# A depthwise convolution split between VectorE and GpSimd: chunks 4 to 6 on GpSimd, two taps a slot on VectorE

## The chip, the core and the metric

The kernel runs on one core of one Trainium2 chip. The metric is device time in microseconds (us) of one launch, the median of three runs. The core's engines are TensorE (PE in the profile), VectorE (DVE), ScalarE (ACT), GpSimd (POOL) and SyncE (SP), which issues the DMAs. Each has its own instruction stream; they meet at semaphores alone.

## What is computed

Input x has 16 images of 128 channels and 56x56 pixels, float32. Four layers follow one another, each on the group-normalised x and added to it: a whitening, a deformable convolution (L1), window attention (L2) and a masked 3x3 convolution (L3). The change is in the first steps of L1:

```python
# L1, on x = group_norm(x), N,C,H,W = 16,128,56,56
xproj = inp @ in_w + in_b
x1 = conv_general_dilated(x, dw_w, (1, 1), pad 1, feature_group_count=C)   # depthwise 3x3
x1 = transpose(x1, (0, 2, 3, 1)) + dw_b
mu = x1.mean(-1); var = ((x1 - mu) ** 2).mean(-1)
x1 = gelu((x1 - mu) / sqrt(var + LN_EPS) * ln_g + ln_b)
offset = x1 @ off_w + off_b;  mask = softmax(x1 @ mask_w + mask_b)
out = sample xproj at the offsets, weighted by the mask, @ out_w + out_b
```

In the depthwise convolution each channel is convolved with nine taps of its own.

## The kernel before

An image lies in SBUF with its 128 channels on the partitions and its 3136 pixels along them. It is worked on in 7 chunks (`CHUNKS`) of 8 rows, that is 448 pixels (`CH`).

After a preface (covariance and power iteration, some 500 us), image 0 goes through its first steps alone. Then a loop of 15 turns follows; turn `i` overlaps two images. Its first half is the window stage of image `i` (`windows(i, i + 1)`): 32 slots (`PAIRS`), each with two attention windows on all engines, in an order written out by hand. Between the steps of a slot stand, by slot number, the first steps of image `i + 1`. Its second half is the sampling of image `i + 1` (`sample_tiles`) with the last steps of image `i` between. A last window stage, of image 15, has no next image.

In a window slot VectorE does, in this order: `before_first` (steps of the next image), `shift` (a row maximum and a subtraction of 128x800 from PSUM, lines 1815 and 1817), `turned` (a copy of 128x512 from PSUM, 1824), `normalise` (1831, 1833), `queries_keys` (a copy of 128x400 from PSUM, 1809), `before_last`. TensorE waits for VectorE's copies within the slot, and VectorE for TensorE's results.

The next image's first steps by slot: group norm in slots 2 to 4; its result `vp` (58x58 with a border of zeros) is written by ScalarE in slots 3 to 6, two chunks a slot (line 1135, signal `v1_in`); the projection `xproj` in slots 8 to 11 (PE line 702, VectorE line 1754 the slot after); the depthwise convolution on VectorE; then TensorE takes the channel mean off (`centred`, line 720) in the slots of `CT_AT`, ScalarE copies and squares the result (1115, 1116), the variance follows in slot 18 (`VAR_AT`), the rows go out in slots 20 to 23.

The depthwise convolution is `depthwise(n, j)`, with `j` from 0 to 35. It has four blocks (`DW_BLOCKS`) of two chunks, the last of one: 896, 896, 896 and 448 elements a partition. In each block tap 0 is a `tensor_scalar` (line 1773) from `vp` to `x1c`, and taps 1 to 8 are `scalar_tensor_tensor` (1775): `x1c = vp * w + x1c`, with both tensors in SBUF. `DW_SLOTS` gives three taps to each of the slots 5 to 16: one after `shift`, one after `turned`, one after `queries_keys` (`depthwise_of`, places 0, 1, 2). The block's last tap raises `dw_d`, on which `centred` waits.

GpSimd only writes constants: `zero_windows(i)` at the start of a window stage, `zero_taps` at slots 28 and 32 (line 557, an image's first two tap tables) and in the sampling (561). For image 0 it writes its two tap tables right after the image buffer is zeroed. `Chain` is a helper that raises an engine's own semaphore at each step and waits for it.

Of the kernel before, what the change touches and what calls it, by code (L numbers as in the profile page):

```python
# [8 lines left out]
ALU = mybir.AluOpType  # L9
# [3 lines left out]
N, C, H, W = 16, 128, 56, 56  # L13
PIX = H * W
# [5 lines left out]
G1, P9, CG = 16, 9, 8  # L20
ROWS = 8
CHUNKS = H // ROWS
# [26 lines left out]
TWO = (CHUNKS + 1) // 2  # L49
DW_BLOCKS = (CHUNKS + 1) // 2  # L50
DW_SLOTS = (5, 5, 5) + (6, 6, 6) + (7, 7, 7) + (8, 8, 8) + (9, 9, 9) + (10, 10, 10) + (11, 11, 11) + (12, 12, 12) + (13, 13, 13) + (14, 14, 14) + (15, 15, 15) + (16, 16, 16)
CT_AT = {12: (0, 1), 13: (2, 3), 15: (4, 5), 17: (6,)}

# [60 lines left out]
def build(nc, a):  # L114
    with ExitStack() as ctx:
# [3 lines left out]
        def sem(name):  # L119
            return ctx.enter_context(nc.semaphore(name))  # L120
# [137 lines left out]
        cv = carver(G_AT)  # L258
        x1c = cv(PIX)
        var_rows, sd_rows = cv(CH), cv(CH)  # L260
        sdt = [cv(CH).rearrange("c (t p) -> c t p", t=T4) for _ in range(4)]
# [27 lines left out]
        def sig(name, per=1, prime=PRIME):  # L289
            signals.append(Signal(sem(name), per, prime))  # L290
            return signals[-1]
# [4 lines left out]
        d_init, d_a, d_cov, d_pow, d_pre, d_main, d_blk, d_end = (sem(f"dve_own_{k}") for k in range(8))  # L296
        t_main = sem("act_own_main")

# [21 lines left out]
        cp_col, cp_img = sig("columns_copied", 2 * TY * 16), sig("rows_copied", 2 * 16)  # L320
        dw_d = sig("dw_taps", DW_BLOCKS)
        dw_p, dw_s = sig("dw_psum", CHUNKS), sig("dw_sbuf", CHUNKS)
# [39 lines left out]
        def dw_block(b):  # L362

            return range(2 * b, min(2 * b + 2, CHUNKS))
# [7 lines left out]
        def alone(eng):  # L372
            eng.sem_inc(s_passed, 1)
# [163 lines left out]
        def _(pool):  # L537
# [25 lines left out]
            def zero_windows(i):  # L563
# [11 lines left out]
                for u in range(2):  # L575
                    nc.gpsimd.memset(e_sb[u][:, :, NTOK:], 0.0).then_inc(l2_z.sem, 1)

            zero_taps(None, 0)
            with pool.Fori(0, N - 1) as i:
                zero_windows(i)  # L580
                zero_taps(i, i + 1)
            zero_windows(N - 1)

        @block.tensor
        def _(pe):
# [132 lines left out]
            def centred(n, k, bank):  # L718
                pe.wait_ge(dw_d.sem, dw_d.at(n, k // 2 + 1))
                nc.tensor.matmul(ps[:, bank, 0:CH], centre, x1c[:, k * CH:(k + 1) * CH], start=True, stop=True  # L720
                                 ).then_inc(dw_p.sem, 1)
# [1356 lines left out]
```

## Time and profile before

| what | before |
|---|---|
| time, median of 3 runs | 9815.72 us (9799.69 to 9819.58) |
| the profiled execution | 9807.95 us |
| its span on the core | 9806.1 us |
| busy in the span | PE 82%, DVE 75%, PEld 46%, ACT 40%, POOL 2% |
| granted clock of TensorE, mean | 0.907 |
| first of the 32 slots of the 16 window stages | 864, 1437, 2010, ..., 9435 us |

The profile is of one execution. PE is TensorE's matmuls, PEld its weight loads, beside them. Busy shares are averages over the whole span; in a single stage another engine can be the one that never waits. The chain is followed back from the last instruction, at each step to what released it. A slot is taken here from the start of one copy of line 1824 to the start of the next, so that it holds the second half of one slot's VectorE work and the first half of the next one's.

### The profile page before, as it was taken

Reading aid. Unit: us, or ns where it says so; the run is one execution under the profiler, and the core shown is the slowest. Engines: PE = TensorE matmul, PEld = TensorE weight load, DVE = VectorE, ACT = ScalarE, POOL = GpSimd, SP = SyncE. Lnnn points to the kernel's source line nnn. Section 1 sums busy time; section 2 is a strip of 40 time slices with the busy share of each in tenths; the row PEclk is TensorE's granted clock in tenths of the full one; section 3 lists DMA queues with packets and bytes.
Section 4 is the critical chain, followed back from the end, with each engine's and each line's share of the span. In section 5 each row is a group of like instructions: output and inputs, shape, how many; then the busy total and the mean of one; then the engine's idle time right before and its main releaser. Section 6 shows DMA issues by size and latency. Waiting matters only on the chain.

```text
span 9806.1 us, 288571 instructions
## 1 busy us (share of the span) xinstructions
PE 8025.1 (82%) x123582; PEld 4502.0 (46%) x123582; DVE 7400.9 (75%) x8865; ACT 3946.4 (40%) x6124; POOL 191.2 (2%) x253
## 2 busy tenths in 40 slices
PE   6458888887888888798888878888887988888797
PEld 5324445354444545444453534445353444535354
DVE  2478778868777886878788687878868787886863
ACT  0034435354343535434353533435353343535332
POOL 0000000000000000000000000000000000000000
PEclk7579999998999999899999989999998999999898
DMA  4000201111020111112011111201111110111101
GB/s 116 0 20 22 58 23 48 31 46 42 28 59 23 48 31 46 42 30 58 23 48 30 47 42 32 59 21 47 31 47 42 31 57 22 47 31 46 42 26 53
DMA packets 231836, 391.50 MB, mean 40 GB/s; under 512 B 26736, under 2 KB 168016, under 8 KB 223312
## 3 DMA queue, kind: packets, MB, share of 16 engines
q1 hardware_dynamic: 230544, 372.67, 13.5%
q8 instruction: 1006, 16.48, 0.7%
q14 instruction: 286, 2.34, 0.1%
HBM read 190.38 MB, written 130.55 MB: 33 GB/s over the span
## 4 chain that ended last, share of the span: by engine, by line
PE 58%; DVE 23%; issue 12%; ACT 6%; DVEq 1%; DMA 0%; SPq 0%; POOL 0%; ACTq 0%; POOLq 0%
PE ps L895 11%; PE ps L694 8%; PE ps L760 7%; DVE arena L1720 5%; PE ps L995 4%; PE ps L793 4%; PE ps L985 3%; PE ps L809 3%; PE ps L768 3%; DVE arena L1775 3%; PE ps L716 3%; PE ps L782 2%; DVE arena L1697 2%; DVE arena L1815 1%; DVE arena L1703 1%
## 5 line engine op out<-in xcount | busy, mean ns | idle before, releaser
L895 PE MATMUL ps<-arena,ident 64*64 64x512 f32 x5600 | 1752.1, 679 | 650.3 <-DVE arena L1720 650.1
L897 PE MATMUL ps<-arena,ident 48*64 48x512 f32 x5600 | 1756.0, 680 | 0.0
L1720 DVE TENSOR_TENSOR arena<-arena 112x2560 f32<-112x2560 f32 x560 | 1578.1, 2819 | 95.8 <-PE ps L897 89.3
L895 PEld LDWEIGHTS ps<-arena,ident 64*64 64x64 f32 x5600 | 490.2, 148 | 1686.8 <-issue 1678.0
L760 PE MATMUL ps<-arena,wqk 128*128 128x400 f32 x2048 | 888.3, 551 | 156.1 <-DVE arena L1824 114.4
L694 PE MATMUL ps<-vp,convw 128*128 128x448 f32 x2016 | 822.8, 550 | 23.6 <-ACT vp L1316 23.6
L1703 DVE TENSOR_TENSOR arena<-arena 112x576 f32<-112x576 f32 x1008 | 764.2, 758 | 34.9
L809 PE MATMUL ps<-arena 64*64 64x33 f32 x32768 | 636.7, 226 | 118.5 <-issue 64.5
L1237 ACT ACTIVATE arena<-ps 112x864 f32<-112x864 f32 x224 | 199.2, 889 | 1273.1 <-PE ps L716 1268.4
L793 PE MATMUL ps<-ident,arena 128*128 128x128 f32 x4096 | 575.1, 285 | 142.6 <-ACT arena L1116 43.3
L1815 DVE TENSOR_REDUCE arena<-ps 128x16 f32<-128x800 f32 x512 | 504.9, 986 | 245.3 <-PE ps L782 241.6
L1809 DVE COPY arena<-ps 128x400 f32<-128x400 f32 x512 | 292.8, 572 | 520.8 <-PE ps L760 520.6
L809 PEld LDWEIGHTS ps<-arena 64*64 64x64 f32 x32768 | 567.4, 139 | 218.6 <-issue 217.6
L1697 DVE TENSOR_TENSOR arena<-arena 112x1728 f32<-112x1728 f32 x336 | 655.2, 1950 | 0.2 <-DVE arena L1685 0.2
L768 PE MATMUL ps<-wv,arena 128*64 128x256 f32 x4096 | 572.3, 401 | 37.6 <-ACT arena L1185 37.5
L760 PEld LDWEIGHTS ps<-arena,wqk 128*128 128x128 f32 x2048 | 321.4, 191 | 611.8 <-ACT arena L1172 220.5
L1179 ACT ACTIVATE arena<-arena 128x800 f32<-128x800 f32 x512 | 447.1, 873 | 370.8 <-DVE arena L1817 366.9
L694 PEld LDWEIGHTS ps<-vp,convw 128*128 128x128 f32 x2016 | 365.6, 190 | 457.6 <-issue 433.9
L782 PEld LDWEIGHTS ps<-arena 32*64 32x64 f32 x32768 | 403.0, 135 | 330.9 <-issue 323.1
L793 PEld LDWEIGHTS ps<-ident,arena 128*128 128x128 f32 x4096 | 456.6, 145 | 189.5 <-issue 121.2
L1185 ACT ACTIVATE arena<-ps 128x512 f32<-128x512 f32 x512 | 305.5, 597 | 590.1 <-PE ps L793 589.7
L1775 DVE SCALAR_TENSOR_TENSOR arena<-vp,cols,arena 128x896 f32<-128x896 f32 (+1 forms) x512 | 525.1, 1026 | 1.0
(299 smaller groups left out, 12428.4 us busy)
## 6 DMA issues: line engine op xcount, KB each, us to landing
windows_out<-arena SPq DMA_DIRECT2D x1024, 100.0 KB
arena<-windows_out SPq DMA_DIRECT2D x224, 256.0 KB, 3.9
arena<-windows_out SPq DMA_DIRECT2D x224, 192.0 KB, 3.3
arena<-in_wqk SPq DMA_DIRECT2D x16, 2048.0 KB, 8.2
arena<-in_x_t SPq DMA_DIRECT2D x16, 1568.0 KB, 10.4
arena<-in_x SPq DMA_DIRECT2D x16, 1568.0 KB, 7.3
arena<-arena SPq DMA_DIRECT2D x32, 784.0 KB
out_x<-xb SPq DMA_DIRECT2D x112, 224.0 KB, 2.0
```

The source lines that it names most:

```text
L694: mm = nc.tensor.matmul(ps[:, bank, 0:CH], weights[:, tap, :], vp[:, ROWS * k + dy:ROWS * k + dy + ROWS, dx:dx + W], start=(tap == 0), sto ...
L760: nc.tensor.matmul(ps[:, 5 - m % 2, 0:NWY * NTOK], wqk[:, m * C:(m + 1) * C], xwb[b % 2][:, :, 0:NTOK], start=True, stop=True).then_inc(qk ...
L768: mm = nc.tensor.matmul(ps[hh * SLOT:(hh + 1) * SLOT, 4, wi * 256:(wi + 1) * 256], xwb[b % 2][:, 2 * pr + wi, :], wv[:, hh * 256:(hh + 1) ...
L793: mm = nc.tensor.transpose(ps[:, 4 + q, k * C:(k + 1) * C], e_sb[u][:, 8 * q + 2 * k:8 * q + 2 * k + 2, :], ident)
L809: mm = nc.tensor.matmul(ps[wi * SLOT:(wi + 1) * SLOT, 6 + hh, (kk * 4 + r) * VD:(kk * 4 + r + 1) * VD], et[u][hh * SLOT:(hh + 1) * SLOT, a ...
L895: nc.tensor.matmul(ps[half, 3, :], ident[0:SLOT, 0:SLOT], prod[0:SLOT, ring(c, dy), dx, :], start=(s < 2), stop=(s >= TAPS - 2), skip_grou ...
L897: mm = nc.tensor.matmul(ps[half, 4, :], ident[SLOT:PT, SLOT:], prod[SLOT:PT, ring(c, dy), dx, :], start=(s < 2), stop=(s >= TAPS - 2), ski ...
L1697: ownm.step(V.tensor_tensor(tt[0:PT, :].rearrange("p (a n) -> p a n", a=3), hat[0:PT, :, 0, :], hat[0:PT, bb, 1:2, :].to_broadcast([PT, 3, ...
L1703: ins = V.tensor_tensor(k5, k5, tt[0:PT, aa * HN:(aa + 1) * HN].rearrange("p (x y n) -> p x y n", x=3, y=3), ALU.add)
L1720: V.tensor_tensor(prod[0:PT, ring(c, dy), :, :].rearrange("p k (n e) -> p k n e", e=CG), taps.to_broadcast([PT, SHIFTS, N64, CG]), for_tap ...
L1775: ins = V.scalar_tensor_tensor(acc, around, dww[:, tap:tap + 1], acc, ALU.mult, ALU.add)
L1815: ownb.step(V.tensor_reduce(mxs[u].rearrange("p (r m) -> p r m", r=4), sv, AX.X, ALU.max))
```

## The change

- VectorE keeps blocks 0 and 1 (chunks 0 to 3): 18 taps, two a slot, in slots 5 to 13. Places 0 and 1 are used; nothing stands at place 2.
- GpSimd does blocks 2 (chunks 4 and 5) and 3 (chunk 6) in a new function `depthwise(n)`. It has no multiply and add in one instruction there: a tap is a `tensor_scalar` multiply of `vp` into a scratch tile `dw_part`, then a `tensor_tensor` add of it to `x1c`. That is 9 multiplies and 8 adds a block, 34 instructions an image, each waiting for the one before. It waits for `v1_in` of all seven chunks, and raises `dw_g` at a block's end.
- In GpSimd's stream it stands between `zero_windows(i)` and `zero_taps(i, i + 1)`; for image 0 it stands ahead of `zero_taps(None, 0)`.
- `centred` waits for `dw_d` in chunks 0 to 3 and for `dw_g` in chunks 4 to 6. The centring of chunks 2 and 3 moves from slot 13 to slot 14.

```diff
-DW_BLOCKS = (CHUNKS + 1) // 2
-DW_SLOTS = (5, 5, 5) + (6, 6, 6) + ... + (16, 16, 16)
-CT_AT = {12: (0, 1), 13: (2, 3), 15: (4, 5), 17: (6,)}
+DW_BLOCKS, DW_POOL = 2, 2
+DW_SLOTS = (5, 5, 6, 6, 7, 7, 8, 8, 9) + (9, 10, 10, 11, 11, 12, 12, 13, 13)
+CT_AT = {12: (0, 1), 14: (2, 3), 15: (4, 5), 17: (6,)}
...
+        dw_part = arena[:, G_AT + PIX:G_AT + PIX + 2 * CH]
...
+            def depthwise(n):
+                own_dw.turn(n, 34 - DW_POOL)
+                for b in range(DW_BLOCKS, DW_BLOCKS + DW_POOL):
+                    ks = dw_block(b)
+                    rows, size = ROWS * len(ks), CH * len(ks)
+                    acc = x1c[:, ks[0] * CH:ks[0] * CH + size].rearrange("c (h w) -> c h w", w=W)
+                    part = dw_part[:, 0:size].rearrange("c (h w) -> c h w", w=W)
+                    pool.wait_ge(v1_in.sem, v1_in.at(n, min(ks[-1] + 2, CHUNKS)))
+                    alone(pool)
+                    for tap in range(P9):
+                        dy, dx = tap // 3, tap % 3
+                        around = vp[:, ROWS * ks[0] + dy:ROWS * ks[0] + dy + rows, dx:dx + W]
+                        own_dw.step(nc.gpsimd.tensor_scalar(part if tap else acc, around, dww[:, tap:tap + 1], None, ALU.mult))
+                        alone(pool)
+                        if tap:
+                            ins = nc.gpsimd.tensor_tensor(acc, acc, part, ALU.add)
+                            if tap == P9 - 1:
+                                ins.then_inc(dw_g.sem, 1)
+                            else:
+                                own_dw.step(ins)
+                                alone(pool)
+
+            own_dw = Chain(pool, t_dw)
+            depthwise(0)
             zero_taps(None, 0)
             with pool.Fori(0, N - 1) as i:
                 zero_windows(i)
+                depthwise(i + 1)
                 zero_taps(i, i + 1)
...
             def centred(n, k, bank):
-                pe.wait_ge(dw_d.sem, dw_d.at(n, k // 2 + 1))
+                if k // 2 < DW_BLOCKS:
+                    pe.wait_ge(dw_d.sem, dw_d.at(n, k // 2 + 1))
+                else:
+                    pe.wait_ge(dw_g.sem, dw_g.at(n, k // 2 + 1 - DW_BLOCKS))
```

## Rows read from the trace of the kernel before

**Rows 1.** The page: busy time by engine, and the shares of the chain that ended last.
```profile
PE 8025.1 (82%) x123582; PEld 4502.0 (46%) x123582; DVE 7400.9 (75%) x8865; ACT 3946.4 (40%) x6124; POOL 191.2 (2%) x253
...
PE 58%; DVE 23%; issue 12%; ACT 6%; DVEq 1%; DMA 0%; SPq 0%; POOL 0%; ACTq 0%; POOLq 0%
```

**Rows 2.** Slots 5, 7-9, 11-15, last stage: length; busy PE, PEld, DVE, ACT, POOL.
```profile
3759.84:3767.47 7.63, 6.00 (x152) 3.80 (x148) 7.28 (x10) 4.34 (x8) 0.00 (x0) 1.00 0.10 30
...
3775.00:3781.95 6.95, 6.51 (x156) 4.17 (x152) 6.72 (x9) 4.34 (x6) 0.00 (x0) 1.00 0.12 35
3781.95:3790.59 8.64, 7.33 (x162) 5.66 (x164) 8.47 (x11) 5.04 (x7) 0.00 (x0) 1.00 0.09 26
3790.59:3799.33 8.74, 7.82 (x167) 5.66 (x164) 8.48 (x11) 4.78 (x6) 0.00 (x0) 1.00 0.09 27
...
3807.39:3815.52 8.13, 7.23 (x165) 5.12 (x164) 7.87 (x10) 2.93 (x5) 0.00 (x0) 1.00 0.10 31
3815.52:3823.81 8.29, 7.21 (x152) 4.20 (x150) 7.27 (x9) 4.78 (x8) 0.00 (x0) 1.00 0.09 27
3823.81:3831.49 7.68, 7.00 (x144) 3.83 (x141) 6.58 (x10) 4.19 (x8) 0.00 (x0) 1.00 0.10 29
3831.49:3838.74 7.25, 5.69 (x150) 3.70 (x143) 5.97 (x10) 3.63 (x7) 0.00 (x0) 1.00 0.22 46
3838.74:3847.70 8.96, 7.63 (x174) 4.66 (x173) 5.97 (x10) 4.78 (x9) 0.00 (x0) 1.00 0.60 103
...
9434.66:9615.44 180.78, 167.08 (x4448) 113.01 (x4444) 120.13 (x179) 82.39 (x132) 0.00 (x0) 1.00 0.13 37
```

**Rows 3.** VectorE's timeline around slot 7: start us, us, engine, line, operation.
```profile
3773.83 1.14 DVE L1775 SCALAR_TENSOR_TENSOR arena<-vp,cols,arena 128x896 f32<-128x896 f32 x1
3775.00 0.69 DVE L1824 COPY arena<-ps 128x512 f32<-128x512 f32 x1
3775.61 1.14 DVE L1775 SCALAR_TENSOR_TENSOR arena<-vp,cols,arena 128x896 f32<-128x896 f32 x1
```

**Rows 4.** Groups by shape, VectorE: count, busy us, mean ns, idle before.
```profile
L1775 DVE SCALAR_TENSOR_TENSOR arena<-vp,cols,arena 128x896 f32<-128x896 f32 x384 | 438.6, 1142 | 0.7
...
L1775 DVE SCALAR_TENSOR_TENSOR arena<-vp,cols,arena 128x448 f32<-128x448 f32 x128 | 86.5, 676 | 0.3
...
L1773 DVE TENSOR_SCALAR arena<-vp,cols 128x896 f32<-128x896 f32 x48 | 32.5, 677 | 2.1 <-ACT vp L1135 2.1
```

**Rows 5.** Groups by shape, GpSimd.
```profile
L561 POOL MEMSET arena<- 112x1600 f32 x80 | 114.5, 1431 | 3705.6 <-DVE arena L1720 3705.6
...
L576 POOL MEMSET arena<- 128x224 f32 x32 | 8.1, 286 | 0.0
L567 POOL MEMSET arena<- 128x112 f32 x32 | 5.2, 192 | 1440.0 <-DVEq L1842 1440.0
```

**Rows 6.** Timeline: ScalarE's last chunk of `vp`, and the centring in slots 15 and 17.
```profile
3770.41 0.75 ACT L1135 ACTIVATE vp<-xa,sm 128x448 f32<-128x448 f32 x1
...
3842.26 1.78 PE L720 MATMUL ps<-arena,centre 128*128 128x448 f32 x4
...
3856.02 1.01 PE L720 MATMUL ps<-arena,centre 128*128 128x448 f32 x2
```

**Rows 7.** Timeline: a GpSimd memset, and line 1697 beside it and without one.
```profile
3949.13 1.95 DVE L1697 TENSOR_TENSOR arena<-arena 112x1728 f32<-112x1728 f32 x1
...
3987.73 1.95 DVE L1697 TENSOR_TENSOR arena<-arena 112x1728 f32<-112x1728 f32 x1
...
3987.97 1.43 POOL L561 MEMSET arena<- 112x1600 f32 x1 [41.76 <-DVE arena L1720]
```

**Rows 8.** Timeline of image 0's first steps.
```profile
515.66 4.67 ACT L1135 ACTIVATE vp<-xa,sm 128x448 f32<-128x448 f32 x7 [0.48 <-DVE sm L1558]
...
552.71 5.73 DVE L1775 SCALAR_TENSOR_TENSOR arena<-vp,cols,arena 128x448 f32<-128x448 f32 x8
...
558.58 1.14 PE L720 MATMUL ps<-arena,centre 128*128 128x448 f32 x2 [3.53 <-DVE arena L1775]
```

More of the change, by code:

```diff
@@ L49 @@
 TWO = (CHUNKS + 1) // 2
-DW_BLOCKS = (CHUNKS + 1) // 2
-DW_SLOTS = (5, 5, 5) + (6, 6, 6) + (7, 7, 7) + (8, 8, 8) + (9, 9, 9) + (10, 10, 10) + (11, 11, 11) + (12, 12, 12) + (13, 13, 13) + (14, 14, 14) + (15, 15, 15) + (16, 16, 16)
-CT_AT = {12: (0, 1), 13: (2, 3), 15: (4, 5), 17: (6,)}
+DW_BLOCKS, DW_POOL = 2, 2
+DW_SLOTS = (5, 5, 6, 6, 7, 7, 8, 8, 9) + (9, 10, 10, 11, 11, 12, 12, 13, 13)
+CT_AT = {12: (0, 1), 14: (2, 3), 15: (4, 5), 17: (6,)}
 TOK_Q, TURN_Q, Q2_Q, S2_Q, SOFT_Q, A2_Q, AGG_Q = 2, 6, (8, 10), 12, 15, 18, 20
@@ L296, in build @@
         d_init, d_a, d_cov, d_pow, d_pre, d_main, d_blk, d_end = (sem(f"dve_own_{k}") for k in range(8))
-        t_main = sem("act_own_main")
+        t_main, t_dw = sem("act_own_main"), sem("pool_own_dw")
         a_xt = [sig("a_xt0", 16), sig("a_xt1", 16)]
@@ L320, in build @@
         cp_col, cp_img = sig("columns_copied", 2 * TY * 16), sig("rows_copied", 2 * 16)
-        dw_d = sig("dw_taps", DW_BLOCKS)
+        dw_d, dw_g = sig("dw_taps", DW_BLOCKS), sig("dw_taps_pool", DW_POOL)
         dw_p, dw_s = sig("dw_psum", CHUNKS), sig("dw_sbuf", CHUNKS)
@@ L580, in _ @@
                 zero_windows(i)
+                depthwise(i + 1)
                 zero_taps(i, i + 1)
+            own_dw.end()
             zero_windows(N - 1)
```

## The prediction

> **What bounds the kernel now.** I read the page's busy times and chain first, then the busy time slot by slot in one window stage, then VectorE's timeline there. TensorE is busy 82% and holds 58% of the chain, VectorE 75% and 23%, and GpSimd 2% [rows 1]. The averages mix stages. In the slots in which the convolution stands the picture is another: slot 5 lasts 7.63 us with VectorE busy 7.28, slot 7 6.95 with 6.72, slot 8 8.64 with 8.47, slot 11 8.13 with 7.87 [rows 2]. VectorE is idle 0.1 to 0.4 us a slot from 5 to 11 and sets their length. From slot 12 on it no longer does: 7.27 of 8.29, 6.58 of 7.68, 5.97 of 7.25 and of 8.96; there TensorE waits in turn for the centring, ScalarE's two passes over it and the attention steps. What a slot takes with nothing of a next image in it, the last stage shows: 180.78 us for 31 slots, 5.83 each [rows 2]. So the convolution is on the path in seven slots and beside it in five. For image 0 nothing runs beside it, and every tap is on the path: `vp` is ready at 520.3 (515.66 + 4.67), the last tap ends at 558.4, and the centring follows at 558.58 [rows 8].
>
> **What goes from VectorE.** Blocks 2 and 3: two multiplies (0.68 and about 0.45 us), eight taps of 1.142 and eight of 0.676 [rows 4]: 0.68 + 9.14 + 0.45 + 5.41 = 15.7 us an image, 251 us in 16 images. By slot it is another sum, since the taps are dealt out anew: slots 5 to 13 lose one tap of three, slots 14 to 16 lose three short ones. A tap holds VectorE 1.17 us from its start to the next copy (3773.83 to 3775.00) [rows 3]; I take 1.15. First without any price for GpSimd's work:
> - Slots 5, 6, 7: VectorE stays the bound, at 6.5 us and below, above the 5.83 of a bare slot. 3 x 1.15 = 3.45 us.
> - Slots 8 to 11: TensorE becomes the bound, since it is busy 7.33 and 7.82 us in slots 8 and 9 and 7.23 in slot 11 (slot 10 as 11) [rows 2]; with 0.2 us of gaps they end at 7.5, 8.0, 7.45 and 7.45, a gain of 1.1 + 0.7 + 0.6 + 0.7 = 3.1 us.
> - Slots 12 to 16: VectorE had slack of 0.7 to 3.0 us. Slot 13 gives its centring to slot 14, about -0.9 and +0.7 us (four matmuls and two rounds of ScalarE; both ends unknown, from 0 to 1.5 us each way, and they nearly cancel). The short taps stand between TensorE's results and its next work in part, 0.3 us a slot in four slots. Together 1.4 us.
>
> That is 8.0 us a turn, 119 us in 15 turns.
>
> **What GpSimd's instructions cost.** The trace of before shows no GpSimd instruction that reads SBUF. Its memsets take 0.192 us for 112 elements, 0.286 for 224 and 1.431 for 1600 [rows 5]: 0.84 ns an element and 0.1 us. A block's instruction of 896 elements at that rate is 0.85 us, of 448 it is 0.47. This is the lower end for each of the 34. For the upper end I let every operand pass one after another at that rate: a multiply (one in, one out) twice, 1.70 and 0.95 us, an add (two in, one out) three times, 2.55 and 1.42. Each instruction waits for the one before on a semaphore, for which I add the memset's fixed 0.1 us. Lower end 22.5 + 3.4 = 26 us an image, upper end 9 x 2.65 + 8 x 3.97 + 3.4 = 59 us. I take the multiply at the memset's price and the add at two of them (0.85, 1.70; 0.47, 0.95), nearer to the lower end since the memset is the one row there is: 9 x 1.32 + 8 x 2.65 + 3.4 = 36 us. The Trainium skill, GPSIMD Engine Reference, section 3.1, has 4497 ns for an add of 2048 elements; an estimate from it is 2.0 us for 896, by which the waits below grow by 0.3 us a slot and the forecast by some 15 us. No run here shows it yet.
>
> **Is GpSimd in time?** It starts when the seventh chunk of `vp` lies there, at 3771.2 (3770.41 + 0.75). The centring of chunks 4 and 5 stands at 3842.3, that of chunk 6 at 3856.0 [rows 6]: 71 and 85 us of room, less the 5 to 8 us by which the slots between shrink. With 36 us, and 16 us more if it must let 14 of VectorE's taps of 1.14 pass, it ends at 3823; at the upper end, 59 + 16, at 3846. So its own time is hidden in the 15 turns at both ends. Nothing else waits behind it: its next instruction, the memset of the tap table, belongs to slot 28.
>
> **The two engines together.** VectorE's taps read two SBUF tensors. A one-input multiply of 896 elements takes 0.677 us and a two-input tap 1.142 [rows 4], so VectorE has two read streams from SBUF, and either instruction needs both. What the trace has of a common use is one side only: line 1697, with two SBUF inputs, takes 1.95 us with a GpSimd memset inside it and 1.95 without one [rows 7]. Writing costs nothing; of reading there is no row. The ends are therefore no wait at all and a wait of each tap until the GpSimd instruction in flight is over. I take the second: a multiply and add that both stream their inputs is the case that the row leaves out, and two engines on one resource is what I would plan for. The Trainium skill, SBUF — State Buffer, section Who interferes with whom, says this: a VectorE instruction with two SBUF inputs and a GpSimd instruction that reads SBUF exclude each other for the whole of an instruction, and one that only writes is harmless. By this rule the price is the one below, without it 119 us are gained; the memset row agrees with its second half.
>
> With such a wait, per slot, while block 2 runs: the first tap meets an instruction at a random point. The mean rest is half the mean square over the mean, (9 x 0.72 + 8 x 2.89) / (2 x 21.3) = 0.69, times 0.9 for the gaps: 0.65 us. The second tap starts 0.6 us after the first has ended (a copy stands between [rows 3]), when GpSimd has just begun one: 0.25 us are left of a multiply, 1.1 of an add, 0.65 in the mean. 1.3 us a slot, while one tap less gives back 1.15. Block 2 takes 23 us of its own and 9 us of let-pass, to about 3803, so slots 7 to 10; slot 11 to 13 have block 3, with half of it.
> - Slots 5 and 6, before GpSimd starts: -2.3 us.
> - Slots 7 to 10: +0.15 each, +0.6 us.
> - Slot 11: -0.6 us. Slots 12 to 16: the waits fall into slack, -1.3 us.
>
> -3.6 us a turn, 15 turns: -54 us.
>
> **Image 0.** Here GpSimd's time is on the path from 520.3 on. VectorE's 15 taps that are left run beside it and block it for 15 x 1.14 = 17 us: 520.3 + 36 + 17 = 573, against 558.4: +14 us. The lower end is +5 (26 + 17 = 43), the upper +38 (59 + 17 = 76). The two memsets that now stand behind it are needed only some 30 us after the centring.
>
> **Sum.** -54 + 14 = -40 us. The profiled execution's 9808 us become 9768; it is 8 us under the median of 9816, which becomes 9776 us.
>
> **Rivals.**
> - *No exclusion.* VectorE's taps and GpSimd's instructions run side by side as the memset did [rows 7]. -119 us, image 0 about 0 (520.3 + 36 = 556): 9697 us. For it: the one row of overlap. Against it: the memset reads nothing.
> - *Long locks: slower.* The same wait at the upper prices. First tap (9 x 2.89 + 8 x 6.50) / (2 x 35.7) x 0.9 = 0.98, second tap 1.5: 2.5 us a slot; slots 7 to 11 +1.35 each, slots 5 and 6 -2.3, the rest -1.0: +3.5 us a turn, +52, and +38 for image 0: 9906 us. It turns from gain to loss where the mean wait of a tap in slots 7 to 11 passes about 0.9 us, that is with an add of some 2.3 us. For it: every operand passes one read port in turn. Against it: nothing but the memset's rate.
> - *GpSimd late.* If its 34 instructions take over 79 us with VectorE's taps let pass (a third more than the upper end), each turn waits at the centring of chunk 6. At 1.3 times the upper prices 14 us a turn are missing: +210, with the locks above over 10,100 us. Against it: the room in [rows 6].
> - *Gain without an effect.* The change frees slots 5 and 6 as said, but slots 8 to 13 give the same back; that is the middle between the first two cases, within 20 us of before.
>
> **Numbers.** No more than 0.2% (20 us) can be told from no change. Short locks, my forecast, 45%, of which 8 points end within 20 us of before. No exclusion 15%. Long locks 34%, of which 6 points within 20 us. GpSimd late 6%. Faster 37 + 15 = 52%, same 14%, slower 28 + 6 = 34%. The likeliest case's own range, from the lower prices (waits of 0.6 us a slot, -96 + 5 us) to an add at two and a half memset prices (some 20 us more than forecast), is 9725 to 9800. The range for 8 in 10 goes from no exclusion to the long locks: 9690 to 9900.
>
> **What the profile after would show.** VectorE busy near 7150 us (7401 - 251), if locks aren't counted into an instruction, and more if they are; line 1775 at 896 elements with a mean over 1.142, or a new idle time before it. GpSimd busy 700 to 1100 us. A multiply at 0.85 and an add at 1.70 us; the two by themselves decide between the cases. Slots 5 and 6 at 6.4 us in each case; slots 7 to 10 between 7.1 and 8.9 with short locks, at 7.5 to 8.0 (slot 7 5.8) with none, at 8.3 to 10 with long ones. No wait of line 720 for GpSimd but in image 0, where the last centring stands near 573. The prediction is wrong if taps are not delayed while GpSimd reads, if its instructions cost over 2.3 us, or if TensorE waits for `dw_g` in a turn.

## The result and the profile after

The changed kernel takes 9851.85 us (median of 7 runs, 9838.79 to 9861.74) against 9815.72 for the kernel before (7 runs on the same chip, 9798.89 to 9839.58). The ratio is 1.0036 [1.0023, 1.0049]: 36 us slower, more than can be confused with no change. The forecast was 9776 us. The profiled execution took 9851.85 us, its span is 9850.0, against 9806.1 before.

Line numbers have moved by 30 for VectorE (the tap is L1805, the copy at a slot's start L1854, the two reads of the scores L1845 and L1847), by 30 for the centring of TensorE (L750) and by 30 for ScalarE (`vp` L1165, the squares L1145 and L1146). The new GpSimd lines are L591 (multiply) and L594 (add).

The page: busy time, and the chain that ended last.

```profile
PE 7999.7 (81%) x123582; PEld 4496.3 (46%) x123582; DVE 7249.7 (74%) x8577; ACT 3949.9 (40%) x6124; POOL 1270.3 (13%) x797
...
PE 59%; DVE 21%; issue 11%; ACT 6%; POOL 1%; DVEq 1%; DMA 0%; SPq 0%; ACTq 0%; POOLq 0%
```

VectorE lost 151 us of busy time ([rows 1] has 7400.9), not 251: waits that the change brings are counted inside the instructions that wait (of the 100 us that are missing 72 are longer taps and first multiplies, 70 of them in the long taps, 256 x 0.275; most of the rest is a matter of counting, since busy time counts the overlap of two VectorE records once, and records overlap by 254 us in all before and 232 after). GpSimd went from 191 to 1270 us. In the chain VectorE has 2 points less, TensorE and GpSimd have one more each.

Groups by shape, GpSimd first, then VectorE's taps and its first multiplies (count, busy us, mean ns, idle before and its releasers):

```profile
L591 POOL TENSOR_SCALAR arena<-vp,cols 128x896 f32<-128x896 f32 x144 | 397.3, 2759 | 990.0 <-ACT vp L1165 963.8 <-POOL arena L594 23.1 <-POOL arena L591 3.2
L594 POOL TENSOR_TENSOR arena<-arena 128x896 f32<-128x896 f32 x128 | 306.4, 2394 | 23.5 <-POOL arena L591 23.5
L591 POOL TENSOR_SCALAR arena<-vp,cols 128x448 f32<-128x448 f32 x144 | 225.3, 1564 | 27.5 <-POOL arena L594 24.3 <-POOL arena L591 3.2
L594 POOL TENSOR_TENSOR arena<-arena 128x448 f32<-128x448 f32 x128 | 150.0, 1172 | 23.5 <-POOL arena L591 23.5
...
L1805 DVE SCALAR_TENSOR_TENSOR arena<-vp,cols,arena 128x896 f32<-128x896 f32 x256 | 362.8, 1417 | 0.4
L1803 DVE TENSOR_SCALAR arena<-vp,cols 128x896 f32<-128x896 f32 x32 | 23.6, 739 | 2.1 <-ACT vp L1165 2.1
```

The four GpSimd groups sum to 1079 us, 67.4 an image. A long tap's mean went from 1.142 [rows 4] to 1.417 us, with no idle time before it: a tap that is held by GpSimd shows as a longer tap.

Slots 5, 7 to 9, 11 to 15 of one window stage (length; busy PE, PEld, DVE, ACT, POOL, each with its count of instructions; then the granted clock, the DMA share and GB/s), to set against [rows 2]:

```profile
4924.52:4930.88 6.36, 5.77 (x152) 3.80 (x148) 6.13 (x9) 4.23 (x7) 0.00 (x0) 1.00 0.12 35
...
4938.41:4945.24 6.83, 6.52 (x156) 4.17 (x152) 6.61 (x8) 4.69 (x6) 6.44 (x3) 1.00 0.12 35
4945.24:4954.84 9.60, 7.72 (x164) 5.66 (x164) 8.77 (x11) 5.39 (x7) 8.82 (x5) 1.00 0.08 23
4954.84:4963.14 8.30, 7.41 (x164) 5.61 (x164) 7.28 (x12) 4.21 (x5) 7.73 (x4) 1.00 0.10 27
...
4972.84:4980.42 7.58, 7.40 (x164) 4.93 (x160) 6.92 (x10) 2.58 (x4) 7.01 (x4) 1.00 0.11 33
4980.42:4989.81 9.39, 7.00 (x150) 4.25 (x150) 7.33 (x8) 4.89 (x8) 8.62 (x6) 1.00 0.08 24
4989.81:4995.03 5.22, 4.81 (x134) 3.19 (x130) 5.06 (x8) 1.70 (x3) 4.62 (x4) 1.00 0.06 16
4995.03:5002.59 7.56, 6.65 (x124) 3.68 (x117) 4.05 (x8) 5.45 (x10) 6.60 (x6) 1.00 0.37 77
5002.59:5010.91 8.32, 7.48 (x172) 4.51 (x176) 4.12 (x8) 4.93 (x9) 5.58 (x5) 1.00 0.61 108
```

Slot 5 is shorter by one tap (7.63 to 6.36), as forecast. Slot 8, in which GpSimd runs, is longer with one tap less (8.64 to 9.60), and slot 12 too (8.29 to 9.39). The slot that gained most is slot 13, 7.68 to 5.22; there the forecast had a gain of 0.9 us from the centring, and little from the taps. From the first to the last instruction the difference of the two traces divides thus (worked out from the times of the slots' first copies): up to the first slot of the first window stage +29.0, the 15 window stages with a next image -15.6, from the last multiply of the sampling to the next stage's first slot +30.0, the sampling -6.9, the last stage and the tail +7.4; together +44.

### The profile page after: what moved, and what is told of

Read it like the earlier page. It is cut to its first block, busy times and chain, and to the rows that moved or that the text cites. A ratio compares the mean times of both kernels' runs of the same rounds, so it can differ in the third digit from the quotient of the medians.

```text
span 9850.0 us, 289525 instructions
## 1 busy us (share of the span) xinstructions
PE 7999.7 (81%) x123582; PEld 4496.3 (46%) x123582; DVE 7249.7 (74%) x8577; ACT 3949.9 (40%) x6124; POOL 1270.3 (13%) x797
## 4 chain that ended last, share of the span: by engine, by line
PE 59%; DVE 21%; issue 11%; ACT 6%; POOL 1%; DVEq 1%; DMA 0%; SPq 0%; ACTq 0%; POOLq 0%
PE ps L925 11%; PE ps L721 7%; PE ps L790 7%; DVE arena L1750 5%; PE ps L1025 4%; PE ps L823 4%; PE ps L1015 3%; PE ps L812 3%; PE ps L839 3%; PE ps L798 3%; PE ps L743 3%; DVE arena L1805 2%; DVE arena L1845 2%; DVE arena L1727 1%; DVE arena L1733 1%
## 5 line engine op out<-in xcount | busy, mean ns | idle before, releaser
L591 POOL TENSOR_SCALAR arena<-vp,cols 128x896 f32<-128x896 f32 (+1 forms) x288 | 622.6, 2162 | 1017.5 <-ACT vp L1165 963.8
L1845 DVE TENSOR_REDUCE arena<-ps 128x16 f32<-128x800 f32 x512 | 505.8, 988 | 307.3 <-PE ps L812 301.6
L562 POOL MEMSET arena<- 112x1600 f32 x80 | 114.5, 1431 | 3647.1 <-DVE arena L1750 3647.1
```

The costliest lines, as they stand in the source:

```text
L1845: ownb.step(V.tensor_reduce(mxs[u].rearrange("p (r m) -> p r m", r=4), sv, AX.X, ALU.max))
```

## Experiments

Kernel 1 is the kernel of experiment 1, and so on. Each time is the median of the kernel's runs; each ratio is to the kernel before on the same chip, with its 95% interval. The kernel before had medians of 9815.9, 9821.6 and 9826.5 us on the three chips used. The sampling's length varies by up to 29 us between profiled executions of kernels that have the same sampling code (4712.7 us in kernel 4, 4741.4 in kernel 9), so medians carry the totals, and the traces only say where. Sums over slots 5 to 16 are per turn, means of the 15 turns of one trace.

**1. GpSimd's part left out.** In the turns blocks 2 and 3 are made by nobody and TensorE doesn't wait for them; image 0 is convolved by VectorE alone.

```diff
-                depthwise(i + 1)
...
-                else:
+                elif isinstance(n, int):
                     pe.wait_ge(dw_g.sem, dw_g.at(n, k // 2 + 1 - DW_BLOCKS))
...
-                for place in range(3):
-                    depthwise_of(s, 0, place)
+                for j in range(36):
+                    if DW_FIRST[j] == s:
+                        depthwise(0, j)
```

> Left out: the depthwise convolution of chunks 4 to 6 of images 1 to 15 (GpSimd does nothing of it, TensorE does not wait for it); image 0 has all 36 taps on VectorE. VectorE keeps its 18 taps at two a slot. Theory A (the window stage gained 1.0 us a turn and not 8 because VectorE's taps wait while GpSimd reads SBUF): the window stage of a turn gets 6 to 8 us shorter than before, and its 16 long taps are 1.142 us each. Rival B (the freed VectorE time was never on the path, TensorE and ScalarE set the slots): 1 to 3 us shorter, as in the changed kernel. Theory C (2 us a turn are lost after VectorE's branch over the far-sampling code, because its program has another length): the gap behind that branch is near 0.5 or near 2.8 us, not between, whatever GpSimd does. Time by A: 9816 - 110 to - 120, with the long gap + 30: 9700 to 9735. By B: 9780 to 9820.

Measured: 9742.82 us (4 runs), 0.993 [0.9911, 0.9948], just outside what theory A gave (at most 9735 us, and at least 6 us a turn), and well away from B. The trace is that of the fastest run (9721.35). In it the window stages are 83.9 us shorter than before, 5.6 a turn; slots 5 to 16 take 88.95 us in place of 94.21. Slots 5, 8, 9, 11, 12 and 13 of one stage:

```profile
4854.10:4860.45 6.35, 5.85 (x154) 3.85 (x150) 6.12 (x9) 4.23 (x7) 0.00 (x0) 1.00 0.12 35
...
4874.39:4882.74 8.35, 8.08 (x170) 5.79 (x166) 7.52 (x10) 4.77 (x6) 0.00 (x0) 1.00 0.10 29
4882.74:4891.06 8.32, 7.69 (x168) 5.61 (x164) 7.24 (x12) 4.79 (x7) 0.00 (x0) 1.00 0.10 28
...
4899.52:4907.16 7.64, 7.47 (x164) 4.99 (x162) 6.92 (x9) 2.57 (x4) 0.00 (x0) 1.00 0.11 33
4907.16:4915.45 8.29, 6.83 (x150) 4.20 (x150) 6.22 (x8) 4.79 (x8) 0.00 (x0) 1.00 0.09 27
4915.45:4920.61 5.16, 5.01 (x142) 3.27 (x140) 5.00 (x8) 1.70 (x3) 0.00 (x0) 1.00 0.07 19
```

So freeing VectorE is worth 5.3 us a turn in slots 5 to 16, not 8.0, even at no price. In slot 8 VectorE has 0.83 us of idle time now and before had 0.17, and the slot is only 0.29 shorter: one tap (1.14) went, and VectorE now waits for TensorE's projection in the middle of the slot instead:

```profile
4876.67 2.22 PE L727 MATMUL ps<-inw,arena 128*112 128x128 f32 x16
...
4877.84 0.69 DVE L1782 TENSOR_TENSOR arena<-ps,inb_row 112x512 f32<-112x512 f32 x1 [0.20 <-PE ps L727]
...
4878.93 0.69 DVE L1782 TENSOR_TENSOR arena<-ps,inb_row 112x512 f32<-112x512 f32 x1 [0.40 <-PE ps L727]
```

The two brackets are VectorE's idle time before the instruction and who ended it. Before, the third tap stood in that place, right ahead of the same two instructions, and they followed it without idle time (slot 8 of the stage of [rows 2]):

```profile
3785.12 1.14 DVE L1775 SCALAR_TENSOR_TENSOR arena<-vp,cols,arena 128x896 f32<-128x896 f32 x1
3786.29 1.29 DVE L1754 TENSOR_TENSOR arena<-ps,inb_row 112x512 f32<-112x512 f32 x2
```

It filled a wait, and taking it out uncovers the wait. Slot 6 shows it more plainly still. The first two rows are of the kernel before, the third is of the changed kernel:

```profile
3770.63 1.14 DVE L1775 SCALAR_TENSOR_TENSOR arena<-vp,cols,arena 128x896 f32<-128x896 f32 x1
3771.89 0.99 DVE L1815 TENSOR_REDUCE arena<-ps 128x16 f32<-128x800 f32 x1
```

```profile
3796.44 0.99 DVE L1845 TENSOR_REDUCE arena<-ps 128x16 f32<-128x800 f32 x1 [1.19 <-PE ps L812]
```

Where the third tap of 1.14 us stood, VectorE now waits 1.19 us for TensorE's scores. The slot lasts 7.54 us before, 7.54 in the changed kernel and 7.53 in kernel 1, wherever TensorE's granted clock is 1.00 in it: nothing is gained.

The clock is in these means too. In the kernel before, 6 of the 15 slots 6 ran at a lower granted clock, 8.40 us at 0.59 in one turn. With only the slots at a granted clock of 1.00, slots 5 to 16 sum to 93.65 us before, 88.83 in kernel 1, 92.84 in kernel 2, 90.05 in kernel 5 and 92.48 in the changed kernel. So 4.8 us a turn is what the missing taps give back, and the rest up to 5.3 goes with the clock.

**2. Image 0 by VectorE alone**, the turns as in the changed kernel. The edit is the last part of the one above, with GpSimd's call for image 0 taken out.

```diff
             own_dw = Chain(pool, t_dw)
-            depthwise(0)
             zero_taps(None, 0)
```

> The changed kernel, but image 0 has all 36 taps on VectorE in the slots of before; GpSimd does blocks 2 and 3 from image 1 on. The stretch up to the first window slot goes back from 893 to 864 us: 29 us less, 9852 to 9823. If only half of it comes back (say 15 us), something else than GpSimd's 71 us on image 0's path made the first stretch longer. VectorE's program gets 18 taps longer ahead of the loop: by theory C the gap behind its skip branch may flip to 0.5 us, which would take another 30 us (9793).

Measured: 9820.51 us (10 runs), 0.9998 [0.9987, 1.0009], on the same chip as kernels 1, 3 and 4. The first window slot starts at 861.52 us, 31.5 earlier than in the changed kernel. Against kernel 1 GpSimd's work in 15 turns is added, and nothing else: +77.7 us, 5.2 a turn. Against kernel 4, which is the changed kernel with its code shifted (9852.19 us on this chip), it is -31.7 us, the size of image 0. The changed kernel itself differs from kernel 2 in two ways more, which experiment 4 is about.

**3. The kernel before, with GpSimd's 34 instructions added.** VectorE keeps all its taps; GpSimd runs as many multiplies and adds of the same sizes into the scratch tile, and the centring waits for it. Both inputs of its adds are the scratch tile.

```diff
+            def depthwise(n):
+                own_dw.turn(n, 34)
...
                 pe.wait_ge(dw_d.sem, dw_d.at(n, k // 2 + 1))
+                if k >= 4:
+                    pe.wait_ge(dw_g.sem, dw_g.at(n, k // 2 - 1))
```

> The kernel before with all its 36 taps on VectorE and with GpSimd's 34 instructions an image besides, into a scratch tile (multiplies read vp, adds read the scratch tile twice); the centring of chunks 4 to 6 waits for both. VectorE's program is that of before to the instruction. Theory A: each tap that falls into an add waits for its rest, so the window stage gets 6 to 10 us longer a turn, the taps' mean goes from 1.142 to about 1.45 us; with image 0 (29 us and more) 9930 to 10000. Rival B (no price of running beside each other worth naming): image 0 alone, 9845 to 9855. Theory C: the gap behind the skip branch stays at 0.5 us, since VectorE's program has not changed.

Measured: 9926.74 us (4 runs), 1.0108 [1.0088, 1.0129], +111 us. Before the first window slot +32.3, the window stages +73.3, 4.9 a turn. Expected were 6 to 10 us a turn and 9930 or more; it is a little under both. Slots 5 to 16 grew by 5.3 us (99.50 from 94.21), where the same comparison of kernels 2 and 1 gives 4.9. So the price of GpSimd's presence is about the same whether VectorE's share is small or whole. It is not quite the same work: an add whose two inputs are one tile takes 1.68 us undisturbed at 128x896, against 2.07 in the changed kernel.

**4. A shift of the code.** The changed kernel with 59 semaphore increments on VectorE ahead of image 0's sampling.

```diff
                 before_last(s, 0)
+            for _ in range(59):
+                alone(dve)
             sample_tiles(0, None)
```

> The changed kernel with 59 semaphore increments on VectorE, once, ahead of image 0's sampling: as many instructions as the change took from its program up to the loop's skip branch, which so lies at the address of before. Theory C (where the code lies decides how long VectorE waits for instructions after the branch): the gap goes from 2.8 back to 0.5 us in the 15 turns, the time from 9852 to about 9825 (30 us less, 3 us more for the increments). Rival (the branch is slow because of what GpSimd or a DMA does at that time): nothing changes, 9855.

What it asks: after the last multiply of a turn's sampling VectorE takes the branch at L2035 (L2005 before), and it begins its next work 2 us later than in the kernel before. The waits of VectorE for "issue" (total us, count, longest) in the kernel before, the changed one, and this one:

```profile
DVE w0s L1734 <- issue: 70.1, 15, 5.2
```

```profile
DVE w0s L1764 <- issue: 100.4, 15, 7.8
```

```profile
DVE w0s L1764 <- issue: 69.6, 15, 5.3
```

The 30 us are in the row of the changed kernel and gone with the shift: from the branch to the next instruction it is 0.53 us before, 2.92 after, 0.53 here, with the same instructions (0.4 of the 2.4 us comes back at the branch that follows). Yet the time is 9852.19 us (5 runs), 1.0038 [1.0024, 1.0053], the same as the changed kernel. The increments cost 8 us, and the window stages are 30 us longer than in the changed kernel. So the branch's 30 us are real, and taking them away doesn't bring the time back. Kernel 2 doesn't have them either (0.53), its window stages are 29 us longer too (3446.4 against 3417.3), and so it is faster by the size of image 0 alone.

Part of where the window stages grew: one turn's slot 13 and another turn's, in this kernel.

```profile
2138.00:2143.21 5.21, 4.80 (x134) 3.19 (x130) 5.05 (x8) 1.70 (x3) 4.62 (x4) 1.00 0.06 15
2708.60:2716.71 8.11, 8.11 (x192) 5.45 (x188) 5.24 (x8) 1.70 (x3) 7.12 (x6) 0.72 0.10 28
```

The same slot, with the same VectorE instructions, lasts 5.21 us at a granted clock of 1.00 and 8.11 at 0.72. TensorE's work in it isn't the same: 192 matmuls in place of 134, most of them left over from slot 12, which has 113 in place of 150 at a granted clock of 0.88. Over slots 12 to 14 together it is 22.16 us and 24.79. Summed over the window stages of the 15 turns, TensorE has 190 us at 1.2 GHz in the changed kernel, 244 here, 249 in kernel 2, 147 in kernel 1 and 211 before. 55 us more at half the speed are worth up to 27 us, which is the size of the 30. That is agreement in size, not proof: which comes first, the shift of the waits or the clock, these runs don't tell.

**5. Multiplies in place of the adds**, else as kernel 2. The sum of the taps of chunks 4 to 6 is left out.

```diff
-                            ins = nc.gpsimd.tensor_tensor(acc, acc, part, ALU.add)
+                            ins = nc.gpsimd.tensor_scalar(acc, part, dww[:, tap:tap + 1], None, ALU.mult)
```

> As e2 (image 0 on VectorE), but each of GpSimd's 16 adds an image is a second multiply of the scratch tile into x1c; left out is the sum of the taps of chunks 4 to 6 for images 1 to 15. Theory A, in the form that the changed kernel's trace gives it (a multiply of 896 elements takes 2.52 us but keeps VectorE from its second input for the first 0.8 us only, an add for all of its 2.07 us but the last 0.2): the taps' mean falls from 1.38 to under 1.22 us, slots 8, 10 and 12 lose most of what they had over the kernel without GpSimd's work, slots 5 to 16 take 89.5 to 91 us against 93.9 in e2 and 89.0 without GpSimd; 9745 to 9785 us. Rival (the wait is for any GpSimd instruction in flight): the taps' mean stays at 1.38 or rises, since the multiplies are longer than the adds; 9820 us or more.

Measured: 9758.17 us (6 runs), 0.9942 [0.9923, 0.9962]. GpSimd is about as busy (1238 us, 1207 in kernel 2), and slots 5 to 16 take 90.16 us in place of 93.87. The groups that took the add's place, and VectorE's taps:

```profile
L595 POOL TENSOR_SCALAR arena<-arena,cols 128x896 f32<-128x896 f32 x120 | 318.9, 2658 | 24.1 <-POOL arena L592 24.1
...
L1805 DVE SCALAR_TENSOR_TENSOR arena<-vp,cols,arena 128x896 f32<-128x896 f32 x264 | 319.9, 1212 | 0.7
```

A tap is 1.381 us in kernel 2, 1.212 here and 1.143 without GpSimd. Of the 4.9 us a turn that slots 5 to 16 lose to GpSimd (93.87 - 88.95) 3.7 go with the adds; 34 multiplies, which take longer, cost 1.2. Among slots at a granted clock of 1.00 it is 2.8 of 4.0, and 1.2.

**6. The second tap of a slot put later**, behind the queries' and keys' copy, else as kernel 2.

```diff
-                    if n is not None:
-                        depthwise_of(s, n, 1)
...
                     if n is not None:
+                        depthwise_of(s, n, 1)
                         depthwise_of(s, n, 2)
```

> As e2, but the second tap of a slot stands after VectorE's copy of the queries and keys and not after the copy of the turned exponentials. If what costs is that a waiting tap holds up the copy for which TensorE waits, slots 8 to 12 get shorter by 0.3 to 1 us each and the time falls by 20 to 50 us under e2's 9820. If only VectorE's sum counts, it stays within 10 us of e2. It can also go up: the tap then stands right before the row maximum of the scores.

Measured: 9911.42 us (4 runs), 1.0103 [1.0081, 1.0125], 1.05% over kernel 2 by the two ratios; the gain that was expected first didn't come. Slots 5 to 16 take 99.73 us; slot 10 alone is 3.18 longer than before and slot 7 1.97. A tap's mean rose from 1.381 to 1.533 us; over the 264 taps that is 2.7 us a turn of the 5.9 by which slots 5 to 16 grew against kernel 2. Some of the rest goes with the clock (335 us at 1.2 GHz in the window stages, 249 in kernel 2); the remainder is put down here to the order itself, two taps one after the other ahead of the reads of the scores, and no run takes the two apart. So where a tap stands matters as much as GpSimd's presence, and the place of the changed kernel is the better of the two.

**7. Only the last chunk by GpSimd**, 27 taps by VectorE (three a slot but in slots 5, 11 and 13), image 0 by VectorE.

```diff
-DW_BLOCKS, DW_POOL = 2, 2
+DW_BLOCKS, DW_POOL = 3, 1
```

> A smaller split: VectorE does chunks 0 to 5 (27 taps, two in slots 5, 11 and 13, three in slots 6 to 10, 12 and 14), GpSimd chunk 6 alone (9 multiplies of 1.40 us and 8 adds of 1.13, some 25 us from slot 7 to 10), image 0 all on VectorE. By theory A the price of the adds is small (8 of 1.13 us, in which three or four taps wait 0.5 us), while slots 5, 11 and 13 keep what the two-tap slots gained: slots 5 to 16 2 to 3 us under before, 9770 to 9790 us. If a third tap in slots 6 to 10 with GpSimd beside it costs its full 1.15 us, it is at 9810 or above.

Measured: 9836.24 us (10 runs), 1.0018 [1.0005, 1.003], not the 9770 to 9790 of the first expectation. Slots 5 to 16 take 94.04 us, as before. Half of the instructions of GpSimd doesn't help: slot 5 gains its tap (-1.27) and slot 13 -1.32, and slots 7 and 9, with three taps beside GpSimd, give back 1.97 and 0.99.

**8. and 10. A small delay in each turn**: 15 semaphore increments of VectorE at the start of each window stage, in kernel 2 and in the kernel before.

```diff
                 if n is not None:
+                    for _ in range(15):
+                        alone(dve)
                     whitening(n)
```

> As e2, with 15 semaphore increments on VectorE at the start of each turn's window stage, 2 us in all, where the changed kernel lost 2 us behind its skip branch. If 2 us lost at that place are a loss of 2 us a turn: 9820 + 30 = 9850. If the rest of the turn takes them up (in e4 the gap went and the time stayed; the window stage got longer by as much, in slots in which TensorE's clock was at 1.2 GHz), the time stays at 9820 within 10 us.

> The kernel before with the 15 semaphore increments of e8 on VectorE at the start of each turn's window stage (0.8 us there, 12 us in all). A control for how far a shift alone moves the time by the slots that TensorE spends at 1.2 GHz: with no such effect +12 us, 9830; by what e8 and e4 showed the window stage can answer with up to 25 us either way, 9800 to 9855.

Measured: 9813.44 us (10 runs), 0.9997 [0.9985, 1.0008], and 9833.68 us (12 runs), 1.0004 [0.9995, 1.0013]. The increments took 0.8 us a turn and not the 2 us meant. In the first kernel the window stages became 36.9 us shorter than in kernel 2, with 168 us at 1.2 GHz in place of 249; in the second they stayed (-0.8) with 149 in place of 211. In both pairs, and in the changed kernel against kernel 4, the kernel in which VectorE is late at the start of the window stage has 54 to 81 us less at 1.2 GHz, in one trace each. But a delay of some 12 us in all can be paid back or not, so the low clock's time is not the whole of it. Neither run could be told from its kernel without the delay.

**9. VectorE alone, with the taps dealt by what experiment 1 showed.** The kernel before, no GpSimd work; slots 5, 11 and 13 get two taps, slot 15 five, slot 16 four, the rest three, dealt in order over a slot's three places; the centring of chunks 2 and 3 moves to slot 14.

```diff
-CT_AT = {12: (0, 1), 13: (2, 3), 15: (4, 5), 17: (6,)}
+DW_SLOTS = (5,) * 2 + (6,) * 3 + ... + (11,) * 2 + (12,) * 3 + (13,) * 2 + (14,) * 3 + (15,) * 5 + (16,) * 4
+CT_AT = {12: (0, 1), 14: (2, 3), 15: (4, 5), 17: (6,)}
```

> The kernel before, without GpSimd's part: all 36 taps on VectorE, but dealt out by what a third tap cost in the slots of the kernel without GpSimd's work against before (slot 5 1.3 us, slot 11 0.6, slot 13 1.2 with its centring; slots 6 to 10 and 12 under 0.5): two taps in slots 5, 11 and 13, three in 6 to 10, 12 and 14, five short ones in 15, four in 16; the centring of chunks 2 and 3 moves from slot 13 to 14. If the gain of the two-tap slots is a matter of where the taps stand and not of who makes them, slots 5 to 16 take 1.5 to 2.5 us less a turn than before: 9780 to 9800 us. If the taps put off to slots 15 and 16 cost as much there, nothing: within 10 us of before.

Measured: 9798.1 us (7 runs), 0.9972 [0.9961, 0.9984]: faster than both kernels. Slots 5, 13 and 15 of one stage:

```profile
4902.40:4908.75 6.35, 5.76 (x152) 3.81 (x148) 6.12 (x8) 4.22 (x7) 0.00 (x0) 1.00 0.12 35
4965.53:4971.88 6.35, 6.08 (x156) 3.92 (x152) 6.12 (x8) 2.58 (x4) 0.00 (x0) 1.00 0.12 35
4980.19:4989.21 9.02, 8.06 (x160) 4.58 (x156) 7.25 (x12) 4.89 (x8) 0.00 (x0) 1.00 0.60 107
```

Slot 5 has the gain of the change (6.35) without GpSimd, slot 13 half of it, and five short taps in slot 15 lengthen it from 8.96 [rows 2] to 9.02. Slot 14, which has its three taps and the centring too, grows from 7.25 to 8.31. Slots 5 to 16 take 92.23 us in place of 94.21, as expected (1.5 to 2.5 us less).

## Why the forecast missed

The forecast was faster by 40 us, and the kernel is slower by 36; it lies inside the wide range, 9690 to 9900, but on the other side of the kernel before. By medians the +36 us is a sum of three. The pairs of the first two rows differ in that alone, with what the clock did in each. The changed kernel differs from kernel 2 also in the 30 us at the branch and in window stages 29 us shorter; in the traces these two cancel, and the first window slot by itself starts 31.5 us later:

| term | forecast | measured | pair |
|---|---|---|---|
| less work for VectorE, no price | -119 | -73 | kernel 1 against before |
| GpSimd beside it in 15 turns | +65 | +78 | kernel 2 against kernel 1 |
| image 0 | +14 | +31 | the changed kernel against kernel 2 |
| sum | -40 | +36 | |

Mean lengths of slots 5 to 16 over the 15 turns, in us:

| slot | 5 | 6 | 7 | 8 | 9 | 10 | 11 | 12 | 13 | 14 | 15 | 16 |
|---|---|---|---|---|---|---|---|---|---|---|---|---|
| before | 7.63 | 7.96 | 6.97 | 8.64 | 8.73 | 8.05 | 8.22 | 8.29 | 7.68 | 7.25 | 8.71 | 6.08 |
| kernel 1 | 6.35 | 7.53 | 6.65 | 8.35 | 8.31 | 8.46 | 7.59 | 8.29 | 5.16 | 7.46 | 8.28 | 6.51 |
| after | 6.36 | 7.54 | 6.87 | 9.68 | 9.00 | 9.44 | 7.92 | 9.11 | 5.19 | 7.53 | 8.27 | 6.46 |

**The gain without a price: the step that failed most (46 of the 76 us).** The forecast said of slots 5 to 7 "VectorE stays the bound", 1.15 us each. True of slot 5 (-1.28); slot 7 gained 0.32, and slot 6 0.43 in the mean, but nothing at a granted clock of 1.00 (experiment 1). Slot 6 lasts 7.67 us in the last stage of the kernel before, where there is no next image at all: the 5.83 us that the forecast took for a bare slot [rows 2] is a mean over 31 slots that run from 2.94 to 7.67, and the one slot in question is the longest of them. For slots 8 to 11 the forecast took TensorE's busy time plus 0.2 us of gaps as the floor, 7.5 to 8.0; they end at 8.35, 8.31, 8.46 and 7.59, 0.9 us of gain a turn and not 3.1. Busy time isn't the floor where two engines wait for each other in turn, as the timeline of kernel 1's slot 8 shows. Only slots 12 to 16 gave more than forecast (2.3 us, not 1.4), all of it by slot 13, which lost its centring and its third tap together while slot 14 took the centring for 0.2. Together 5.3 us a turn in place of 8.0.

**GpSimd's prices: mis-sized, and the multiply by three.** A stretch of one turn, GpSimd and then VectorE (start, us, instruction; in brackets the idle time before and its releaser):

```profile
4370.85 2.11 POOL L594 TENSOR_TENSOR arena<-arena 128x896 f32<-128x896 f32 x1 [0.18 <-POOL arena L591]
4373.16 2.52 POOL L591 TENSOR_SCALAR arena<-vp,cols 128x896 f32<-128x896 f32 x1 [0.21 <-POOL arena L594]
4375.87 2.07 POOL L594 TENSOR_TENSOR arena<-arena 128x896 f32<-128x896 f32 x1 [0.18 <-POOL arena L591]
4378.15 3.13 POOL L591 TENSOR_SCALAR arena<-vp,cols 128x896 f32<-128x896 f32 x1 [0.21 <-POOL arena L594]
```

```profile
4373.34 0.99 DVE L1847 TENSOR_TENSOR arena<-ps,arena 128x800 f32<-128x800 f32 x1
4374.25 1.14 DVE L1805 SCALAR_TENSOR_TENSOR arena<-vp,cols,arena 128x896 f32<-128x896 f32 x1
4375.43 0.69 DVE L1854 COPY arena<-ps 128x512 f32<-128x512 f32 x1
4376.04 2.86 DVE L1805 SCALAR_TENSOR_TENSOR arena<-vp,cols,arena 128x896 f32<-128x896 f32 x1
4378.93 0.26 DVE L1861 RECIPROCAL arena<-ps 128x16 f32<-128x16 f32 x1
```

Undisturbed, the multiply takes 2.52 us and the add 2.07 (forecast 0.85 and 1.70), with 0.2 between two (0.1). The multiply is over the 2.3 us from which the forecast called itself wrong; at 448 elements, as the rows of image 0 below show, the two take 1.40 and 1.13 (0.47 and 0.95). An image is 9 x 3.92 + 8 x 3.20 + 34 x 0.2 = 67.7 us, not 36, and over the upper end of 59. The memset's rate was no guide to instructions that read. The rule weighed in the forecast, the Trainium skill, GPSIMD Engine Reference, section 3.1, was right for the add (2.0 us estimated, 2.07 measured). The Trainium skill, GPSIMD Engine Reference, section 4.1, says that a one-input instruction runs roughly at line rate; the trace disagrees with it for this multiply, 2.52 us against 0.68 for VectorE's [rows 4].

**In time for the centring: right, with less to spare.** GpSimd is done with block 3 at about 4437.7 in that turn, 12 us ahead of the centring of chunk 6 at 4450.03; over the 15 turns the margin is 11 to 19 us, where the forecast had some 25. TensorE waits for GpSimd in image 0 alone. The rival "GpSimd late" is out. (The forecast put the threshold of this rival at 79 us with the waits and also at a third more than the upper end; 59 + 16 is 75, so the two don't agree, and the first was the nearer one.)

**The exclusion: the mechanism was right, the size nearly.** The tap at 4376.04 met the add of 4375.87, which ends at 4377.94, and lasted 2.86 us: 1.72 too long, so it ran from 0.19 us before the add's end. The tap at 4374.25 started 1.09 us into a multiply of 2.52 and wasn't held at all. Over the 240 long taps of the changed kernel's 15 turns, those that started in an add (64) waited 0.86 us in the mean, those in a multiply (104) 0.07, the other 72 next to nothing: 63.8 us in all, 4.25 a turn. Only taps that began in the first 0.8 us of a multiply waited, and until that point. The forecast had a mean wait of 0.65 us in block 2 for both kinds; it is 0.27 over all taps, since the multiply, which is over half of GpSimd's time, keeps a tap waiting only at its start. That the sum still came out near (+65 forecast, +78) is luck, two errors that cancel: half the wait, in instructions that last twice as long and so reach over slots 6 to 15, where block 2 was forecast for slots 7 to 10 and block 3 for 11 to 13 (the forecast's own start, 3771.2, lies in slot 6 [rows 2], not behind it). Slot 12, where waits were to fall into slack, grew by 0.82. The Trainium skill, SBUF — State Buffer, section Who interferes with whom, gives the lock for the whole of an instruction: so it is for adds, and experiment 5 and the waits above (0.07 us in the mean) show that it isn't for multiplies.

**Image 0: the price of GpSimd on the path.** First and last instructions, and what TensorE and ScalarE waited for:

```profile
516.90 2.60 POOL L591 TENSOR_SCALAR arena<-vp,cols 128x896 f32<-128x896 f32 x1 [17.02 <-ACT vp L1165]
...
585.52 1.40 POOL L591 TENSOR_SCALAR arena<-vp,cols 128x448 f32<-128x448 f32 x1 [0.20 <-POOL arena L594]
587.10 1.13 POOL L594 TENSOR_TENSOR arena<-arena 128x448 f32<-128x448 f32 x1 [0.18 <-POOL arena L591]
...
588.38 1.83 PE L750 MATMUL ps<-arena,centre 128*128 128x448 f32 x2 [21.39 <-POOL arena L594]
590.24 0.63 ACT L1145 ACTIVATE arena<-ps,cols 128x448 f32<-128x448 f32 x1 [22.07 <-PE ps L750]
```

GpSimd works from 516.90 to 588.2, and the last centring starts at 588.38 and not at 573; before it was 558.58 [rows 8]. That GpSimd's time is on the path stood in the forecast, and the 15 us between 573 and 588 are a sum of three: GpSimd's own work took 31.7 us more than forecast (67.7, not 36), it lost 3.6 us to VectorE's taps and not 17, and it started 3.4 us before the 520.3 of the kernel before.

**The sum.** With the gain of kernel 1 (-73) and the measured image 0 (+31), the forecast's own +65 for the turns gives +23: the side of slower. The rival "long locks" (9906 us, an add of 2.55) turned where the mean wait of a tap passes 0.9 us; the add is 2.07, the mean wait 0.27, and it isn't what happened. Three of the slots 7 to 10 (9.68, 9.00, 9.44) do lie in the 8.3 to 10 that the forecast gave for long locks, but kernel 1 has 8.35, 8.31 and 8.46 there with no GpSimd work at all. Nearest is the rival "gain without an effect", in which slots 8 to 13 give back what slots 5 and 6 free: kernel 2, which is the change without its cost in image 0, is at 0.9998 of the time before. It came out so by other sums, since slot 6 freed nothing and slot 13 gained 2.5 us.

**Left open.** Why a multiply keeps VectorE waiting only in the first third of its time. And what moves TensorE's stretches at 1.2 GHz: in the window stages they differ by up to 81 us between kernels whose work is the same (kernels 2 and 8), enough to cover effects of 20 to 40 us in a single pair of traces. So it isn't shown either that the 30 us at the branch and the 29 us of the window stages belong together; that they cancel may be chance.

## What to carry to other kernels

Before you count an instruction's time as a gain, look at what the next one waits for once it is gone: of 8.0 us a turn 5.3 were there. Where the trace has the same step without its neighbour's work, as slot 6 in the last stage, take the floor from that step and not from a mean; where two engines wait for each other, busy time is no floor. Work given to GpSimd beside VectorE instructions that read two SBUF tensors was paid for in VectorE's waits (15.7 us of VectorE's work a turn, taken away, bought 5 us, and the waits cost 5), so first deal VectorE's own work anew; kernel 9 did that and gained 0.28%. And a step that is hidden in every turn but runs bare in the first image has to be priced there too: that alone was 31 of the 36 us.

## What the runs showed of the hardware

- GpSimd's multiply by a scalar of each partition is slower than its add of two tensors: 2.52 against 2.07 us at 128x896, 1.40 against 1.13 at 128x448.
- The exclusion works both ways. Of the changed kernel's multiplies at 128x896, the 54 that started while a tap ran took 3.15 us in the mean and the other 90 2.52; of its adds, the 52 that did took 2.81 and the others 2.11.
- An add whose two inputs are the same tile takes 1.68 us, one with two tiles 2.07 (128x896, undisturbed; experiment 3 and the changed kernel).
- The same instructions at another place of the code: 0.53 us from a taken branch to the next instruction, or 2.92 us (experiment 4), and this flipped with edits elsewhere.
- Slots 12 to 14 took 22.16 us in one turn, at a granted clock of 1.00, and 24.79 in another, with 0.72 in slot 13 (experiment 4).
